# The f16 high halves of the probabilities all on ScalarE, four tiles for the last normalisation, and new instruction lists

## The reference

```python
def attn(x, Wqkv, Wo):                     # B=4, S=512, D=512, H=16, HD=32
    q, k, v = split(x @ Wqkv)
    scores = einsum('bhqd,bhkd->bhqk', q, k) * HD ** -0.5
    a = softmax(where(causal, scores, -1e9))
    return merge(einsum('bhqk,bhkd->bhqd', a, v)) @ Wo

x = x + attn(layernorm(x), Wqkv, Wo)
y = layernorm(x)
x = x + (silu(y @ w1q.T) * (y @ w3q.T)) @ w2q.T      # w?q = clip(round(w / mean|w|), -1, 1) * mean|w|
```

## Time and profile before

| | |
|---|---|
| median of 3 runs | 563.12 us (562.99 to 564.51) |
| the profiled execution, its time | 564.71 us |
| its span, first to last instruction | 562.9 us |
| busy in the span: PE, DVE, ACT, POOL | 502.1, 407.7, 359.5, 340.8 us |

### The profile page before, as it was taken

One profiled execution on the slowest core, in us unless ns is written; L12 is line 12 of the kernel. 1 busy time (PEld: TensorE's weight loads), 2 busy tenths in 40 slices (PEclk: granted clock), 3 DMA queues, 4 the chain that ended last, 5 costly groups with the idle time before them and its releaser, 6 DMA issues. The chain is left out here.

```text
span 562.9 us, 11519 instructions
## 1 busy us (share of the span) xinstructions
PE 502.1 (89%) x4092; PEld 230.4 (41%) x4092; DVE 407.7 (72%) x1102; ACT 359.5 (64%) x885; POOL 340.8 (61%) x365
## 2 busy tenths in 40 slices
PE   2697665777999999999989999999979999999997
PEld 1343222233444444544444444444434444444443
DVE  7797787597998996675875869776979985433322
ACT  4898989778848687756556686665468884113320
POOL 3086699477775986845764776655567886233220
PEclk9999855797999999999998999999989999999999
DMA  8949979999798787366778556468496858230002
GB/s 311 352 81 235 222 179 226 225 191 169 138 154 178 141 153 131 73 116 163 156 114 181 82 95 113 87 140 184 108 160 114 151 95 153 90 93 1 1 1 93
DMA packets 224206, 79.52 MB, mean 141 GB/s; under 512 B 213226, under 2 KB 213226, under 8 KB 224148
## 3 DMA queue, kind: packets, MB, share of 16 engines
q1 hardware_dynamic: 224148, 78.79, 68.3%
HBM read 20.97 MB, written 4.19 MB: 45 GB/s over the span
## 5 line engine op out<-in xcount | busy, mean ns | idle before, releaser
L674 POOL TENSOR_TENSOR early<-early 128x512 f16<-128x512 f32 (+1 forms) x192 | 195.0, 1025 | 102.4 <-ACT early L783 75.9
L773 ACT ACTIVATE early<-early,exp_bias 128x512 f32<-128x512 f32 (+3 forms) x256 | 140.8, 551 | 49.3 <-DVE exp_bias L994 48.7
L1146 PE MATMUL work<-late,w_ternary 128*128 128x512 f16 (+1 forms) x704 | 161.0, 385 | 8.1 <-DMA late<-rows 6.8
L985 DVE CUSTOM_DVE_ANT_0 early<-score_bank,mask,scalars 128x512 f32<-128x512 f32 (+3 forms) x256 | 132.8, 544 | 33.1 <-POOL early L674 17.8
L1146 PEld LDWEIGHTS work<-late,w_ternary 128*128 128x128 f16 (+1 forms) x704 | 68.6, 101 | 91.7 <-issue 14.7
L1146 PE MATMUL work<-xt,wqkv_hi 128*128 128x512 f16 x256 | 81.5, 402 | 4.7 <-DVE o_sb L1024 2.3
L1309 PE MATMUL work<-w_ternary,late 128*128 128x512 f16 (+1 forms) x352 | 78.1, 379 | 0.0
L692 POOL TENSOR_TENSOR late<-late 128x512 f16<-128x512 f32 (+1 forms) x44 | 50.8, 1159 | 43.2 <-ACT late L810 43.1
L1004 DVE CAST early<-early 128x512 f16<-128x512 f32 (+1 forms) x96 | 55.4, 577 | 22.9 <-ACT early L773 17.8
L783 ACT ACTIVATE early<-early 128x512 f16<-128x512 f32 (+1 forms) x96 | 52.6, 550 | 9.5 <-DMA early<-early 5.2
L803 ACT ACTIVATE late<-work,scalars 128x512 f32<-128x512 f32 (+1 forms) x44 | 29.8, 678 | 39.2 <-PE work L1146 20.4
(11 more groups left out here) (108 smaller groups left out, 729.4 us busy)
## 6 DMA issues: line engine op xcount, KB each, us to landing
rows<-in_L_attn_x SPq DMA_DIRECT2D x16, 256.0 KB, 3.1
x_res<-in_L_attn_x SPq DMA_DIRECT2D x12, 256.0 KB, 3.1
out_y<-x_res SPq DMA_DIRECT2D x12, 256.0 KB, 2.2
late<-in_L_ffn_w SPq DMA_DIRECT2D x4, 682.5 KB, 5.0
early<-in_L_ffn_w SPq DMA_DIRECT2D x3, 768.0 KB, 12.6
late<-in_L_ffn_w SPq DMA_DIRECT2D x3, 768.0 KB, 5.6
late<-in_L_attn_Wqkv SPq DMA_DIRECT2D x4, 512.0 KB, 6.6
late<-in_L_attn_Wqkv SPq DMA_DIRECT2D x1, 1024.0 KB, 9.9
```

The lines of the kernel that those rows point to most:

```text
L674: pool.tensor_tensor(split_view(s, p, 1, h), raw_view(s, p, h), split_view(s, p, 0, h), ALU.subtract).then_inc(low_done, 1)
L773: last = act.activation(piece, piece, ACT.Exp, bias=bias, accum_out=sums[:, s % 2, at:at + 1])
L985: last = dve.tensor_tensor_reduce(raws[n % RAWS][:, off:off + cols], score_bank[h][:, off:off + cols], mask[:, S - cols:S], scalar(exp_sca ...
L1146: last = pe.matmul(bank, lhs, rhs, start=(n == 0), stop=(n == len(terms) - 1))
```

## The change

Three things.

1. All 192 `high` steps are ACT's; DVE's list has none.
2. In the last batch, `norm_y` of row blocks 2 and 3 writes into the two tiles of x, which are no longer used by then. It then waits for x's last turn and not for the turn of y's blocks 0 and 1.
3. All five lists are laid anew. PE, POOL and SP have the same steps as before in another order; ACT has 96 more, DVE 96 fewer. (The loop in `turn_rows` over PSUM banks now names only the banks that occur.)

```diff
+        def y_tile(b, i):
+            return "x" if b == BATCHES - 1 and i > 1 else "y"
...
             def turn_rows(step):
...
-                    for n_bank in range(NW):
+                    for n_bank in sorted({bank_of(r) for r in readers}):
...
+                at = "x" if n == "x" else y_tile(b, i)
                 sp.dma_start_transpose((xt if n == "x" else yt)[:, :, i * P:(i + 1) * P],
-                                       split_rows[n][i % 2]).then_inc(rows_turned[n][i % 2], 16)
+                                       split_rows[at][i % 2]).then_inc(rows_turned[n][i % 2], 16)
...
             def norm_y(b, i):
-                if b or i > 1:
+                if y_tile(b, i) == "x":
+                    dve.wait_ge(rows_turned["x"][i % 2], tiles_turned("x", b, i))
+                elif b or i > 1:
                     before = (b, i - 2) if i > 1 else (b - 1, i + 2)
                     dve.wait_ge(rows_turned["y"][i % 2], tiles_turned("y", *before))
...
     "dve": """
-        pad:w1 stats_x:0,0-3 top_part:0-3 xt:0,0 xt:0,2 xt:0,1 top_turn:qk top_v xt:0,3 split:0-1 top_turn:v
+        pad:w1 top_part:0-2 stats_x:0,0-1 top_part:3 stats_x:0,2 top_turn:qk stats_x:0,3 top_v top_turn:v xt:0,0
```

More of the change, by code:

```diff
@@ L87 @@
[L87 to L91, removed]
@@ L95 @@
+        res_load:3,0-1 yt:3,0-2 down:2,1 yt:3,3 down:3,1 down:2,0 down:3,2 down:2,3 down:2,2 down:3,0 down:3,3
     """,
     "pool": """
[L97 to L100, removed]
@@ L121 @@
[L121 to L125, removed]
@@ L126 @@
[L126 to L145, removed]
@@ L168 @@
+        lin:3,7-8 gate:3,9-10 lin:3,9-10
     """,
     "dve": """
-        pad:w1 stats_x:0,0-3 top_part:0-3 xt:0,0 xt:0,2 xt:0,1 top_turn:qk top_v xt:0,3 split:0-1 top_turn:v
-        split:2-3 weight_mean:w1 wo_max q:0 k:0 split:8 max:0,0,0 stats_x:1,0 max:0,0,1 k:1 bias:0,0,1 max:0,0,2
-        split:4 max:0,0,3 split:5 bias:0,0,3 split:6 high:0,0,1 split:7 top_turn:wo max:0,1,0-1 bias:0,1,1
-        high:0,0,3 pad:w3 max:0,1,2-3 q:1 bias:0,1,3 high:0,1,1 v:0,0 stats_x:1,1 v:0,2 max:0,2,0-1 bias:0,2,1
@@ L224 @@
-        gate:2,8 max:15,2,1 high:15,1,3 bias:15,2,1 lin:2,8 max:15,2,2-3 values:14 bias:15,2,3 high:15,2,1 gate:2,9
-        lin:2,9 high:15,2,3 inverse:15 gate:2,10 lin:2,10 down:2,0 values:15 down:2,1 project:3,0 stats_y:3,0
-        norm_y:3,0 project:3,1 stats_y:3,1 project:3,2 norm_y:3,1 stats_y:3,2 project:3,3 stats_y:3,3 norm_y:3,2-3
+        pad:w1 top_part:0-2 stats_x:0,0-1 top_part:3 stats_x:0,2 top_turn:qk stats_x:0,3 top_v top_turn:v xt:0,0
+        split:0 xt:0,1-3 split:1 weight_mean:w1 wo_max split:2 stats_x:1,0 split:3 stats_x:1,1 q:0 k:0 split:8 k:1
@@ new lines @@
+        max:0,0,0-1 bias:0,0,1 max:0,0,2 split:4 max:0,0,3 split:5 bias:0,0,3 split:6-7 max:0,1,0 top_turn:wo
+        max:0,1,1 bias:0,1,1 max:0,1,2 q:1 pad:w3 v:0,0 max:0,1,3 bias:0,1,3 v:0,1 max:0,2,0-1 v:0,2 bias:0,2,1
+        max:0,2,2-3 bias:0,2,3 wo_split v:0,3 max:1,0,0-1 q:2 weight_mean:w3 bias:1,0,1 max:1,0,2 inverse:0
+        max:1,0,3 bias:1,0,3 max:1,1,0 k:3 max:1,1,1 bias:1,1,1 max:1,1,2-3 bias:1,1,3 max:1,2,0 stats_x:1,2
+        max:1,2,1 bias:1,2,1 values:0 stats_x:1,3 max:1,2,2 k:2 max:1,2,3 bias:1,2,3 q:3 max:2,0,0-1 bias:2,0,1
@@ new lines @@
+        down:0,0 q:10 max:8,1,1 bias:8,1,1 values:7 max:8,1,2-3 down:0,1-2 bias:8,1,3 max:8,2,0 project:1,0
+        max:8,2,1 bias:8,2,1 stats_y:1,0 max:8,2,2-3 down:0,3 norm_y:1,0 project:1,1 bias:8,2,3 stats_y:1,1
+        project:1,2 stats_y:1,2 max:9,0,0-1 bias:9,0,1 max:9,0,2-3 inverse:8 bias:9,0,3 q:11 norm_y:1,1 project:1,3
+        norm_y:1,2 max:9,1,0 stats_y:1,3 max:9,1,1 v:2,0 norm_y:1,3 bias:9,1,1 v:2,1-2 max:9,1,2-3 v:2,3 bias:9,1,3
+        k:11 max:9,2,0-1 gate:1,0 values:8 bias:9,2,1 max:9,2,2-3 lin:1,0 bias:9,2,3 gate:1,1 lin:1,1 stats_x:3,2
```

278 lines of the change are left out of this document (153 added, 125 removed).

## The result

The changed kernel takes 576.84 us (median of 4 runs, 574.54 to 578.87), the kernel before 563.06 beside it: a ratio of 1.0233, 95% interval 1.0199 to 1.0267, so it is slower, clear of the scatter. The profiled execution took 578.87 us with a span of 577.1. The forecast was 573.9 in a range of 559.5 to 581.0.

A forecast was written before the change was run, and what follows sets the result against it. The prediction took ACT to bound slots 0 to 3 and PE the rest. Its terms, +6.1 + 12.1 - 4.3 - 2.8 - 0.3 = +10.8 us, gave 573.9 us against a median of 563.1, range 559.5 to 581.

The forecast's parts named there:

- What bounds: ACT is nearest to full in slots 0 to 3, 88% busy; from 134.4 us on PE sets the time.
- The start, +6.1: Before the first `exp`: `q:0` starts near 27.1 us behind ACT's sums, 6.1 us later, with nothing regained.
- The casts, +12.1 - 4.3 = +7.8: Slots 0 to 3: ACT gets 12.1 us more work, and its waits for DVE's bias take up 4.3.
- Later casts at nothing: From slot 4 on, PE hides DVE's lost casts and 39.6 us of casts added to ACT, at no cost.
- rival three: Slots 4 to 14: ACT sets the time there too and PE waits for gates; 578 to 584 us, chance 0.10.
- PE's late waits, -2.8: After the first `project`: new PE order covers waits for turned y rows in batches 1 and 2, winning 2.8 us.
- Four tiles, -0.3: Last batch: the last two `norm_y` no longer wait 1.34 us for a turn, which wins PE 0.3 us.
- Rival one: Slots 0 to 3: a raw tile's round trip sets the time and shortens without DVE casts; 560 us, chance 0.19.

The follow-up runs named there:

- e8: Kernel before with the new lists for what begins before 36 us, lists of before behind: 568.59 us, ratio 1.0087.
- e13: Lists of before, with only DVE's casts 1 and 3 of slots 0 to 3 moved to ACT: 567.44 us, ratio 1.0087.
- e7: Kernel before with the last batch's blocks 2 and 3 in x's tiles, lists of before: 563.66 us, ratio 0.9988.
- e4: Changed kernel's code with new lists only from 142 us to its 424 us, lists of before on both sides: 564.14 us, ratio 1.0009.
- e12: Kernel before with the new lists from 419 us on, all casts there on ACT: 569.55 us, ratio 1.0104.
- e2: Changed kernel with the lists of before for all that began before 142 us, early casts 1 and 3 on DVE: 567.24 us, ratio 1.0060.
- e14: As e8, with DVE's statistics of batch 0 first again and PE's weight_mean:w1 behind q:0: 571.17 us, ratio 1.0134.
- e1: Changed kernel with the lists of before for what began before 33 us: 576.06 us, ratio 1.0209.
- e3: Changed kernel with the order of before after 424 us, casts 1 and 3 on DVE there: 571.49 us, ratio 1.0138.
- e11: As e3, but with the old end's 15 casts of DVE moved to ACT: 572.83 us, ratio 1.0171.
- e5: Changed kernel with casts 1 and 3 of slots 13 to 15 back on DVE, order otherwise new: 580.03 us, ratio 1.0284.
- e6: Lists of before with every cast of DVE moved to ACT, nothing else moved: 571.99 us, ratio 1.0133.

## Why the prediction was right, and where it was not

In ratios times 563.1 us, each part alone in the lists of before (each of these runs has the four tiles too, so their -0.7 is in every term): start +4.9 (e8), casts of slots 0 to 3 +4.9 (e13), tiles -0.7 with an interval of both signs (e7), new middle +0.5 (e4), new end with its casts +5.9 (e12). Together +15.5, where the whole change has +13.1. Each ratio is uncertain by 0.8 to 1.9 us, so the two agree. The forecast had +10.8.

- **What bounds.** Right. Slots 0 to 3 hang on ACT, and PE has no product to do meanwhile: casts moved to ACT there cost 4.9 us (e13), and start and casts taken back win 9.6 (e2).
- **The start, +6.1.** Right at its place: the sums ended and `q:0` began at 27.18, forecast 27.1, and e14 shows that ACT's order alone holds it until 26.5. DVE's idle time, which is what catches the eye, isn't needed for that. It shrank after that, to 5.2 at the first `exp` and 4.9 at the end of e8; taken back with the casts on ACT it wins only 0.8 by medians (e1). That nothing would be regained ahead of the first `exp` was wrong by 1.0 us.
- **The casts, +12.1 - 4.3 = +7.8.** Right in kind, too large. In the changed kernel ACT has 10.6 us more work between the two `exp` (96.28 against 85.73), not 12.1, and its idle time there went from 11.7 to 4.5 us. So 7.2 us were taken up, not 4.3. The waits for the bias gave 3.2 of it (4.3 to 1.1). The rest came from the waits for turns that I would not count on: that for w1 (2.0) is gone, and those for turned probabilities shrank from 4.2 us to

```profile
ACT early L789 <- DMA early<-early: 2.2, 2, 1.5
```

  My reading, not tested: with more work ahead of it on ACT, a `high` comes up only when its turn has landed. The stretch between the two `exp` grew by 3.5 us, forecast 7.8. At the first `project` the delay is 9.8 us, forecast 13.9, and not all of it is start and casts: in the traces of e8 and e13 `project` is 2.6 and 4.1 us late, together 6.7, while in e2 and e4, without either, it is 3.3 and 5.9 us late.
- **Later casts at nothing.** Right up to slot 13, for casts and new order together (e4, within 0.3%). Wrong in slots 13 to 15, where "PE hides it" was read off a mean over slots 4 to 15. This is the term that the sum lacked: 5.9 us by e12, 5.3 by e3. Part of it is the casts on ACT (1.3 us by the medians of e11 and e3, some 3 by the traces), and part the new order. It stands near my rival three, but ACT's sum of work alone isn't the cause: ACT is busy only 50.0 of the 67.0 us, and e5, which lowers that to 43.6, is no faster. What is on the chain is the turn between `low` and a `high` two fills later. Which of the exchanges in the new order makes that round trip longer was not taken apart.
- **PE's late waits, -2.8.** The waits for turned y rows went from 6.8 to 2.9 us in total (the page's groups of L1154 have 2.9), 3.9 where 2.8 were forecast, and with other gaps the middle wins 4.8 in the trace. The sum left out what the same lists cost at their head: e4, which has them alone, is 5.9 us late at its first `project` and level with before at the end. So the term was worth nothing to the whole.
- **Four tiles, -0.3.** Right, no measurable difference; the wait of 1.34 us is gone (e7).

So the total is near by luck, in part: by the stretches of the trace the forecast has 4 us too much early and 2 too little gain in the middle, and lacks the 9 us of the end (some 6 by e12). The mechanism of the early loss, which the forecast rested on, is the measured one.

Rival one, that the round trip of a raw tile sets slots 0 to 3 and gets shorter without casts on DVE, had the tile right and the sign wrong. The waits of `max` for `low` there went from 9.6 to 23.3 us, and to 27.6 in e13: the `high` that frees the way for `low` now stands in ACT's queue behind its other work.

The Trainium skill (SBUF — State Buffer, "Who interferes with whom") said that casts on DVE can be held up by GpSimd and that ACT waits for no one. The prediction found no row that shows the lock, but the trace of before has it. All 18 full-width casts on DVE of over 700 ns began while a POOL instruction ran, and ended 281 to 287 ns after a POOL instruction did; the 22 that had no POOL instruction beside them took 411 to 428 ns. One of the 18, with its POOL instruction (ends at 122.33 and 122.04 us):

```profile
120.94 1.39 DVE L1004 CAST early<-early 128x512 f16<-128x512 f32 x1
```

```profile
120.86 1.18 POOL L674 TENSOR_TENSOR early<-early 128x512 f16<-128x512 f32 x1 [1.55 <-ACT early L783]
```

The casts on ACT are as the rule has it:

```profile
L789 ACT ACTIVATE early<-early x192: 398/615/632, 44.3 to 480.1; 128x512 f16<-128x512 f32 x128, 128x256 f16<-128x256 f32 x64
```

None takes over 632 ns, where DVE's went up to 2235. As a reason for the change the rule fails on e6: DVE's relief was real (370.0 us busy against 407.7), but it went into longer waits for `low`, on an engine that did not set the time.

No version beat the kernel before; e7 and e4 are level with it.

## What to carry to other kernels

Moving work to an engine that is idle 36% of the span costs time if the stretch in which it lands is the one where that engine is full; read each engine's load by stage, and the last stages apart from the ones with slack. In slots 0 to 3 of this kernel, where ACT stood at 88%, about 60% of its idle time took up new work (7.2 and 6.7 of 11.7 us); that is two readings of one stretch and no rule. Where engines hand tiles round in a circle, work taken off one of them comes back as its waits if the engine that gets it is later: follow the tile and not the busy times. And a stretch that got shorter in the trace is no gain yet: cut it at marks with the same work ahead of them, look whether the stretch ahead of it got longer, and put the part alone into the old kernel.
